# Expert logits from the reads, and one GpSimd chain for two normalisations, in a mixture-of-experts block on one core

## What is computed

```python
    def _L0_ffn_ref(x, gate_w, w1, b1, w2, b2):
        logits = jnp.einsum('bsd,ed->bse', x, gate_w)
        probs = jax.nn.softmax(logits, axis=-1)
        topk_probs, topk_idx = jax.lax.top_k(probs, TOP_K)
        ...
        out = jnp.sum(y * topk_probs[..., None], axis=-2)
        return out
    x = L0_attn_out
    x = x + _L0_attn_ref(_layernorm(x, axis=-1), L0_attn_W_write, L0_attn_W_read, L0_attn_decay, L0_attn_log_alpha)
    x = x + _L0_ffn_ref(_layernorm(x, axis=-1), L0_ffn_gate_w, L0_ffn_w1, L0_ffn_b1, L0_ffn_w2, L0_ffn_b2)
```

## Time and profile before

| | us |
|---|---|
| median of 3 runs | 563.22 (561.47 to 564.38) |
| profiled execution | 562.67 |
| its span in the trace | 560.9 |
| TensorE busy | 530.1 (95%) |
| VectorE busy | 448.4 (80%) |
| ScalarE busy | 338.3 (60%) |
| GpSimd busy | 246.9 (44%) |

### The profile page before, as it was taken

The page is one execution under the profiler, slowest core; times in us unless marked ns, Lnnn a source line. Parts: engine busy times, 40 slices in busy tenths (PEclk is TensorE's granted clock), DMA queues, the critical chain, the costliest instruction groups (busy, mean ns, idle before and its releaser), DMA issues.

```text
span 560.9 us, 17645 instructions
## 1 busy us (share of the span) xinstructions
PE 530.1 (95%) x5234; PEld 415.3 (74%) x5234; DVE 448.4 (80%) x1375; ACT 338.3 (60%) x856; POOL 246.9 (44%) x291
## 2 busy tenths in 40 slices
PE   7799899999999999999999999999999999999991
PEld 7677778778786777777777777777777777777770
DVE  4889999999987689868768787688777777778861
ACT  6899989898745876445545554455544544545540
POOL 5625778888746084523223233223322333322433
PEclk9999999999998999999999999999999999999997
DMA  5576867777345396433263364343344454344323
GB/s 161 201 229 225 258 185 234 210 222 231 126 105 129 87 216 101 71 60 62 51 103 56 53 105 77 63 68 61 61 63 79 78 78 75 68 64 67 63 37 36
DMA packets 85096, 63.33 MB, mean 113 GB/s; under 512 B 54224, under 2 KB 77392, under 8 KB 85008
## 3 DMA queue, kind: packets, MB, share of 16 engines
q1 hardware_dynamic: 71328, 43.94, 32.3%
q0 software_dynamic: 13392, 18.27, 17.3%
q10 hardware_dynamic: 288, 0.00, 0.0%
HBM read 37.56 MB, written 24.62 MB: 111 GB/s over the span
## 4 chain that ended last, share of the span: by engine, by line
PE 77%; DVE 10%; issue 4%; DMA 3%; ACT 2%; POOL 1%; SPq 1%; POOLq 0%; DVEq 0%; ACTq 0%
PE psum L1697 32%; PE psum L1712 21%; PE psum L1714 10%; PE psum L1509 3%; DVE weights L874 2%; PE psum L1592 2%; PE psum L1573 2%; PE psum L1599 2%; PE psum L1520 2%; DVE arena L1052 1%; PE psum L1559 1%; DMA arena<-sent_rows 1%; PE psum L1612 1%; PE psum L1496 1%; DVE arena L1063 1%
## 5 line engine op out<-in xcount | busy, mean ns | idle before, releaser
L1697 PE MATMUL psum<-arena,weights 128*128 128x256 f16 (+1 forms) x2208 | 279.7, 249 | 1.1 <-DVE arena L1316 1.0
L1697 PEld LDWEIGHTS psum<-arena,weights 128*128 x2208 | 187.4, 98 | 79.3 <-issue 4.1
L589 POOL DMA_INDIRECT out<-arena,tile_in x71 | 115.0, 1619 | 233.4 <-DVE arena L1343 126.9
L1712 PE MATMUL psum<-weights,arena 128*128 x556 | 211.7, 381 | 0.0
L826 ACT ACTIVATE arena<-psum,b_cur 128x256 f32<-128x256 f32 (+1 forms) x368 | 131.4, 423 | 129.9 <-PE psum L1697 115.6
L1714 PE MATMUL psum<-weights,arena 128*128 x556 | 152.0, 273 | 0.0
L1327 DVE TENSOR_TENSOR arena<-arena 128x512 f16<-128x512 f32 x142 | 98.5, 694 | 10.8 <-ACT arena L843 6.3
L559 POOL DMA_INDIRECT sent_rows<-arena,tiny x64 | 65.4, 1022 | 35.5 <-issue 17.8
L1323 DVE CAST arena<-arena 128x512 f16<-128x512 f32 x126 | 53.5, 424 | 8.8 <-ACT arena L826 8.5
L1712 PEld LDWEIGHTS psum<-weights,arena 128*128 128x128 f16 x556 | 54.4, 98 | 5.0
L1714 PEld LDWEIGHTS psum<-weights,arena 128*128 128x128 f16 x556 | 54.5, 98 | 4.6
(11 more groups left out here) (199 smaller groups left out, 642.9 us busy)
## 6 DMA issues: line engine op xcount, KB each, us to landing
weights<-in_experts SPq DMA_DIRECT2D x32, 512.0 KB, 4.8
arena<-sent_rows SPq DMA_DIRECT2D x100, 64.0 KB
arena<-in_b SPq DMA_DIRECT2D x46, 128.0 KB, 3.2
arena<-in_x SPq DMA_DIRECT2D x16, 256.0 KB, 3.4
out<-arena SPq DMA_DIRECT2D x16, 256.0 KB, 4.1
arena<-sent_rows SPq DMA_DIRECT2D x84, 32.0 KB
sent_rows<-pad SPq DMA_DIRECT2D x7, 265.0 KB, 4.6
tile_in<-sent_rows SPq DMA_DIRECT2D x71, 4.5 KB, 2.6
```

What stands on the lines that cost most here:

```text
L589: pool.indirect_dma_start(out=out, out_offset=bass.IndirectOffsetOnAxis(ap=at_u, axis=0), in_=yout[:, u % 4], in_offset=None, compute_op=A ...
L1697: last = pe.matmul(ps_h[:, f % 2, mm * n:(mm + 1) * n], w1_of(e_of[i], k, lo, per * (f - GROUP[i]) + mm), turned[:, i % 2, part, k, 0:n], ...
L1712: pe.matmul(to, h_hi[:, z % 4, at], w2_of(e_of[t], m), start=(m == 0), stop=(m == MF - 1), skip_group_check=True)
```

## The change

The logits no longer come from the second normalised rows. Since a row's mean and factor are the same for all its channels, they are a per-row factor times x1 times the gate with each expert's mean over the channels taken off (the centred gate). x1 times that gate splits in two: the reads times (W_read.T times the gate), which becomes eight more columns of `project`; and x + xn, which is a per-row factor (`sides`) times xn, so xn in f16 halves times the gate in f16 halves (`gate_x`), scaled by ScalarE (`scale_gate`). VectorE adds the two. The second factor goes into the exponential as its scale. So logits, choice and scatter come one step earlier (`LAG = 4`), and `turn_normed`, `score_experts` and `normed_transposed` are gone. At the start four small steps prepare the gate: `mean_gate`, `centre_gate`, `gate_in_halves`, `gate_through_reads`, `read_gate`, and one more load of 256 KB, W_read by rows.

GpSimd's two chains become one, of four columns instead of two, which waits for the first moments of chunk n and for the second of chunk n-3. Two small instructions (`roots`, `sides`) follow it.

The diff, cut to what the prediction speaks of:

```diff
-LAG = 5
+LAG = 4
...
+            sp.dma_start(gateT[:], gate_w).then_inc(gate_in, 16)
             sp.dma_start(third_x, both(x_rows, 2)).then_inc(third_in, 16)
             sp.dma_start(ww_words, w_write.rearrange("p k d -> p (k d)")).then_inc(proj_in, 16)
-            sp.dma_start(wrT[:], w_read).then_inc(read_in, 16)
-            sp.dma_start(gateT[:], gate_w).then_inc(gate_in, 16)
-            sp.dma_start(b1T[:], b1).then_inc(gate_in, 16)
+            sp.dma_start(wr_rows, w_read_rows).then_inc(rows_in, 16)
+            sp.dma_start(wrT[:, :, 0:D], w_read).then_inc(read_in, 16)
+            sp.dma_start(b1T[:], b1).then_inc(b1_in, 16)
...
-                        pool.tensor_scalar(ve, moments[:, :, 1], EPS, None, ALU.add)
-                        pool.tensor_scalar(shift, moments[:, :, 0], -1.0, None, ALU.mult).then_inc(S[mid], 1)
-                        reached(pool, mid, m)
-                        pool.tensor_tensor(rs, ve, minus_half[:].to_broadcast([P, B]), ALU.pow).then_inc(S[end], 1)
-                        reached(pool, end, m)
-                        pool.tensor_tensor(shift, shift, rs, ALU.mult).then_inc(S[last], 1)
-                if active(n, 5):
-                    m = n - 5
+                if active(n, 0) or active(n, 3):
+                    both_kinds = slice(0 if active(n, 0) else B, 2 * B if active(n, 3) else B)
+                    count = both_kinds.stop - both_kinds.start
+                    if active(n, 0):
+
+                        reached(pool, "moments1_done", n)
+                        reached(pool, "res_done", n - 2)
+                    if active(n, 3):
+
+                        reached(pool, "moments2_done", n - 3)
+                        reached(pool, "xm_done", n - 5)
+                        reached(pool, "exp_done", n - 5)
+                    got, ve = moments_all[:, both_kinds], variances[:, both_kinds]
+                    rs, shift = factors[par][:, both_kinds], shifts[par][:, both_kinds]
+                    pool.tensor_scalar(ve, got[:, :, 1], EPS, None, ALU.add)
+                    pool.tensor_scalar(shift, got[:, :, 0], -1.0, None, ALU.mult).then_inc(S["taken"], 1)
+                    reached(pool, "taken", n)
+                    pool.tensor_tensor(rs, ve, minus_half[:].to_broadcast([P, count]),
+                                       ALU.pow).then_inc(S["factors_done"], 1)
+                    reached(pool, "factors_done", n)
+                    pool.tensor_tensor(shift, shift, rs, ALU.mult).then_inc(S["shifts_done"], 1)
+                if active(n, 0):
+                    reached(pool, "gate_x_done", n - 4)
+                    pool.tensor_tensor(roots[:], variances[:, 0:B], rs1[par], ALU.mult).then_inc(S["root_done"], 1)
+                    reached(pool, "root_done", n)
+                    pool.tensor_scalar(sides[:, n % 4], roots[:], 1.0 / WSCALE, 1.0 / WSCALE, ALU.mult,
+                                       ALU.add).then_inc(S["side_done"], 1)
+                if active(n, 4):
+                    m = n - 4
...
+            def scale_gate(m):
+
+                reached(a, "gate_x_ps", m)
+                reached(a, "state_done", min(m, NCH - 2))
+                reached(a, "side_done", m)
+                reached(a, "logit_done", m - 1)
+                for b in range(B):
+                    last = a.activation(gate_x_part[:, b], ps_gate_x[:, b], ACT.Copy, scale=sides[:, m % 4, b:b + 1])
+                last.then_inc(S["gate_x_done"], 1)
 
...
-                a.activation(shifted, shifted, ACT.Exp).then_inc(S["exp_done"], 1)
+                reached(a, "factors_done", m + 3)
+                for b in range(B):
+                    last = a.activation(shifted[:, b], shifted[:, b], ACT.Exp, scale=rs2_of(m)[:, b:b + 1])
+                last.then_inc(S["exp_done"], 1)
...
-                if active(n, 5):
-                    exponential(n - 5)
+                if active(n, 3):
+                    scale_gate(n - 3)
+                if active(n, 4):
+                    exponential(n - 4)
...
             def logits(m):
 
-                reached(v, "logit_ps", m)
+                reached(v, "proj_ps", m)
+                reached(v, "gate_x_done", m)
                 reached(v, "top_at_done", m - 1)
-                v.tensor_copy(logit, ps_logit).then_inc(S["logit_done"], 1)
+                v.tensor_tensor(logit, ps_gate_read, gate_x_part[:], ALU.add).then_inc(S["logit_done"], 1)
...
                 if active(n, 3):
                     residual(n - 3)
+                    logits(n - 3)
+                if active(n, 3):
+                    residual_stats(n - 3)
+                    residual_moments(n - 3)
                 for j in splits(n)[0:1]:
                     split_low(j)
-                if active(n, 3):
-                    residual_stats(n - 3)
-                if active(n, 5):
-                    weigh_gates(n - 5)
-                if active(n, 3):
-                    residual_moments(n - 3)
+                if active(n, 4):
+                    weigh_gates(n - 4)
                 if active(n, 2):
                     weigh_scores(n - 2)
-                if active(n, 5):
-                    place(n - 5)
                 if active(n, 4):
-                    logits(n - 4)
+                    place(n - 4)
...
+            def centre_gate():
+
+                v.wait_ge(gate_mean_ps, 1)
+                v.tensor_tensor(gateT[:], gateT[:], ps_gate_mean.unsqueeze(1).to_broadcast([P, KD, E]),
+                                ALU.add).then_inc(gate_centred, 1)
+
+            def gate_in_halves():
+
+                v.wait_ge(gate_centred, 1)
+                v.tensor_scalar(gate16[:, 0], gateT[:], WSCALE, None, ALU.mult).then_inc(gate_halves, 1)
+                v.wait_ge(gate_halves, 1)
+                v.scalar_tensor_tensor(out=gate16[:, 1], in0=gateT[:], scalar=WSCALE, in1=gate16[:, 0], op0=ALU.mult,
+                                       op1=ALU.subtract).then_inc(gate_halves, 1)
+
+            def read_gate():
+
+                v.wait_ge(wr_gate_ps, 1)
+                v.tensor_copy(wrT[:, :, D:D + E], ps_wr_gate).then_inc(wr_gate_done, 1)
...
+            def mean_gate():
+
+                pe.wait_ge(gate_in, 16)
+                pe.wait_ge(mean_set, 1)
+                for k in range(KD):
+                    last = pe.matmul(ps_gate_mean, minus_mean, gateT[:, k], start=(k == 0), stop=(k == KD - 1))
+                last.then_inc(gate_mean_ps, 1)
...
+            def gate_through_reads():
+
+                pe.wait_ge(gate_centred, 1)
+                pe.wait_ge(rows_in, 16)
+                for k in range(KD):
+                    for j in range(KD):
+                        last = pe.matmul(ps_wr_gate[:, k], wr_rows[:, j, k * P:(k + 1) * P], gateT[:, j],
+                                         start=(j == 0), stop=(j == KD - 1))
+                last.then_inc(wr_gate_ps, 1)
+
+            def gate_x(m):
+
+                s = m % 2
+                reached(pe, "gate_x_done", m - 1)
+                reached(pe, "state_done", m - 1)
+                reached(pe, "xlo_done", m)
+                if m == 0:
+                    pe.wait_ge(gate_halves, 2)
+                for b in range(B):
+                    for at, (k, x, w) in enumerate(three):
+                        last = pe.matmul(ps_gate_x[:, b], xnT[:, x, s, b, k, 0:P], gate16[:, w, k],
+                                         start=(at == 0), stop=(at == len(three) - 1))
+                last.then_inc(S["gate_x_ps"], 1)
...
+                reached(pe, "logit_done", m - 1)
...
+                        last = pe.matmul(ps_both[:, b], readsT[:, s, b, k, 0:P], wrT[:, k], start=(k == 0),
                                          stop=(k == KD - 1))
                 last.then_inc(S["proj_ps"], 1)
...
+            mean_gate()
             weigh(0)
             values(0)
             reads(0)
             states(0)
+            gate_through_reads()
             full_steps(step, 3)
-            turn_normed(NCH - 3)
+            gate_x(NCH - 2)
             values(NCH - 1)
             weigh(NCH - 1)
             project(NCH - 2)
-            score_experts(NCH - 3)
+            gate_x(NCH - 1)
             reads(NCH - 1)
-            rank(NCH - 4)
+            rank(NCH - 3)
...
             project(NCH - 1)
-            turn_normed(NCH - 2)
             pair(2, None)
-            rank(NCH - 3)
-            score_experts(NCH - 2)
+            rank(NCH - 2)
             pair(3, 0)
-            rank(NCH - 2)
+            rank(NCH - 1)
             pair(4, 1)
-            turn_normed(NCH - 1)
             pair(5, 2)
-            score_experts(NCH - 1)
             pair(6, 3)
-            rank(NCH - 1)
```

188 lines of the change are left out of this document (89 added, 99 removed).

## The result

| | kernel before | changed kernel |
|---|---|---|
| median of four runs | 562.35 us | 576.05 us |
| range of the runs | 559.97 to 564.38 | 571.25 to 577.94 |
| profiled execution, its span | 562.67, 560.9 | 575.97, 573.9 |
| mean granted clock of the profiled execution | 0.990 | 0.967 |

The ratio is 1.0233, 95% interval 1.0191 to 1.0275: slower by 2.3%. The forecast was 564.9 with a range of 559.5 to 569.5, so the result lies outside, within 1 us of a rival that had been given 5%. That its number comes so close is luck, as the account behind the experiments shows: only about half of what was missed is that rival's.

The account below looks back on a forecast made before the run. A loop through four engines was taken to bound stage one's two-piece steps, VectorE its three-piece steps, TensorE stage two. Terms +1.8 +0.5 +0.3 +1.05 -1.85 -0.1 gave +1.7, 564.9 us with the median's 0.55; range 559.5 to 569.5.

Parts of the forecast that it names:

- the clock falls in stage one: Rival: TensorE idle about 1.9 us ahead of reads halves its clock, +1 to +2 in 12 steps, 577 or more; chance 0.05.
- the three-piece steps: Stage-one chunks with three weight pieces, set by VectorE's work: stats and moments wait, 0.17 a step, +0.5 for three.
- the two-piece pitch: Time between residual starts in stage-one steps with two weight pieces: 9.9 us instead of 9.73, +1.05 over seven.
- the handover: From stage one into stage two, TensorE-bound but for a 1.20 us wait: less logit and transpose work, sum -1.85.
- start: Kernel's beginning: transposes behind new gate matmuls +1.2, GpSimd instructions +0.2, first step's logits and chain +0.4; sum +1.8.
- the signs named: Expected in the profile: pitches near 9.9 and 10.6, GpSimd's first instruction over 1 us, TensorE idle 1.5 to 2 us.
- w: Extra cost of GpSimd's power at four columns over two, in its joint chain; taken as 0.35 us.
- R: Start of VectorE's `residual` in a two-piece step; the first low-half split was to end 3.05 us after it.
- r: Start of ScalarE's `reads_high` in a two-piece step; `residual` was to start 2.92 us after it.
- Double power: Rival: GpSimd's four-column power costs twice the two-column 0.71, pitch 10.25, total 568; chance 0.20.
- TensorE's relief: Rival: with less TensorE work, VectorE's bare 9.29 us sets two-piece steps, total 559.5; chance 0.17.
- No dip: Rival: the half-clock stretch at 177 us stays away because rank waits elsewhere, -1.7, total 563.2; chance 0.08.

Follow-up runs that it names:

- two of its gate's matmuls: Changed kernel with ten of `gate_x`'s twelve matmuls left out; ratio 1.0288 to the kernel before.
- the logits moved: Changed kernel with VectorE's logits behind the residual's moments instead of ahead of its statistics; ratio 1.0167 to the kernel before.
- the gaps filled: Changed kernel plus small bf16 matmuls on ones, ten ahead of states and fourteen ahead of reads each full step; ratio 1.0376 to the kernel before.
- the low half moved: Changed kernel with VectorE's first `split_low` behind the placement; ratio to the kernel before 1.0138 (all steps), 1.0175 (two-piece steps only).
- both moves: Changed kernel with logits behind the residual's moments and, in two-piece steps, first `split_low` behind the placement; ratios 1.0059 and 1.0122 to the kernel before.
- the states held: Changed kernel with logits and first low half moved, TensorE's states also waiting until VectorE has weighed the scores; ratio 1.0166 to the kernel before.
- the low half moved and the fill: Changed kernel with the first `split_low` behind the placement in all steps, plus added matmuls ahead of states and reads; ratio 1.0341 to the kernel before.
- the old work put back: Changed kernel plus, each step, four f32 transposes behind project and four 8-column f32 matmuls between states and reads, without waits; ratio 1.0531 to the kernel before.
- the relieved one: Kernel before with half of the normalised rows' transposes and gate matmuls, and the copy between them, left out; ratio 0.9956 to the kernel before.

## Why the prediction was wrong, step by step

**Two steps failed, with about half of the miss each.** The first is the dismissal of "the clock falls in stage one", which I put at 577 or more with a chance of 0.05. I set against it a granted clock of 1.00 in a stretch in which TensorE was busy 45.4 of 51.4 us. That was a mean: before, TensorE's idle time lay in pieces of at most 0.7 us in the two-piece steps, and in that stretch, ahead of the states in its first two steps, in one of 1.29 and one of 0.73, with at most 0.4 elsewhere. The longest, in the kernel before:

```profile
27.28 0.69 PE L1612 MATMUL psum<-arena 128*64 128x64 f32 x16 [1.29 <-ACT arena L693]
```

In the changed kernel's undisturbed two-piece step it lies in two of 0.86 and 1.20 us, 0.69 apart. Among two-piece steps, half-clock stretches were recorded in all profiles but one of the kernels that keep both gaps (the changed kernel, two of its gate's matmuls, the joint chain undone, the logits moved). There were none with the gaps filled, with the low half moved, with both moves, and with the states held as well. But on chips with late results they also came without the two gaps: with the low half moved and the fill, with the old work put back, with twelve matmuls added to the kernel before, and once each in that kernel itself and in the relieved one. That the two gaps bring the clock down is therefore the reading that fits best and not shown; which of TensorE's waits counts stays open. The price was right in kind: at half clock a step took 11.4 to 12.4 us instead of 10.19.

The second is the sum itself, without any fall. The five disturbed pitches of the profiled execution are 11.45, 11.51, 11.35, 12.44 and 11.63; undisturbed, the same pitches are 10.53 and 10.95 (fastest profile), 10.67 (low half moved alone, which leaves the three-piece steps as they are) and twice 10.19. So the falls cost some 5.9 us, and some 7.1 of the 13.0 are there without them; the fastest profile gives 7.3 in the same way (8.6 less 1.3 for its pitches of 11.36 and 11.32). The forecast was +1.7. By this estimate the time without falls would have been about 570.3, still outside the range. The terms that were too small by these 5.4 us are the three-piece steps, the second above all (2.1), the two-piece pitch (2.6) and the handover (0.7), all told below.

**Where the 13 us of the profiled pair went.** The fastest profile (span 569.5, the changed kernel's last run) has no fall in its two-piece steps and serves as the undisturbed one for them.

| step of the sum | forecast | profiled execution | fastest profile |
|---|---|---|---|
| start | +1.8 | +1.80 | +1.43 |
| the next five pitches, the second step's first | +0.5 | +4.75 | +3.66 |
| seven pitches after them | +1.2 | +7.51 | +3.80 |
| last three pitches and all behind | -1.8 | -1.06 | -0.29 |

*Start*: right, and for the reason given, that the transposes wait for `gate_through_reads`: they began at 22.89, ScalarE took them up at 23.55. *`gate_x`* itself was mis-sized: twelve matmuls take 0.46 us, their starts 27 ns apart, not 0.7. The Trainium skill (TensorE: Matmul & The Clock Gate, Wait — 56ns, not 53.3ns?) states that starts never come closer than about 25 ns; the trace agrees, and an estimate by it would have been 0.3 to 0.5.

*The second step* wasn't in the sum. It has three pieces but had taken only 9.26; now 10.53 in the fastest profile, +1.3. ScalarE's `chunk_normalise` (L744) waits there for the joint chain, which waits for the residual's moments, and starts 5.6 us after the residual (31.13 against 25.52); before, its chain needed no residual and it started after 4.0 (28.05 against 24.09). It is the same dependence that I had priced only for two-piece steps.

*Three-piece steps*: 0.17 each forecast; 0.1 and 0.5 in the undisturbed ones of the fastest profile, 0.9 in two with half-clock stretches, which undisturbed take 10.67, 0.25 more than before.

*Two-piece steps*: most of the signs named came, GpSimd's first instruction with 0.97 beside the split, ScalarE's wait of 1.21 for the chain, TensorE idle ahead of the reads. But that idle time was 1.20 us there and 0.86 ahead of the states, where I had 1.5 to 2 in a row; I had not asked what the states wait for. w was 1.04 - 0.72 = 0.32, forecast 0.35. The pitch was 10.19 and not 9.9 by two small terms: `split_low` was left at R + 3.30, not R + 3.05, since stats and moments ended 0.2 later; and R came at r + 3.08, not r + 2.92, since VectorE's queries, and no longer the projection, were last. 0.3 in seven pitches is 2.1 us of error, inside the range by itself.

*Handover and stage two*: I let the wait before the late rank pass as "only lengthens it". It grew from 1.20 to 2.78 us: TensorE's work ahead of it had gone, and VectorE has L1357 (0.68) ahead of the last residual. The dip came again. Of 1.8 us of gain 0.3 to 1.1 came.

**The rivals.** Double power is excluded by 1.04 (twice 0.71 is 1.42). TensorE's relief did not count, for the reason named: the split begins ahead of the chain. No dip: it came. The chances for faster, same and slower don't follow from the list of cases: two thirds of the forecast's 0.50 and the 0.08 make 0.41 for "same", not 0.53, and 0.42 for "slower", not 0.30.

**What stays open** is the second loss, on three of six chips: results 1.7 us late at full recorded clock. It isn't the joint chain (undone, it was still there), and filled gaps with a recorded clock of 1.00 don't keep it away. Both the order of VectorE's work and the amount of TensorE's bear on it: with the low half moved, or both moves, there were no late results; with the low half moved and 24 matmuls a step added, on the same chip, they were back; ten small matmuls fewer took 1.7 to 0.4, twelve more brought them into three steps of the kernel before, and the old work put back left them. That late results follow how much TensorE does at a stretch is a rival to the order of VectorE's work which no run here decides. Why TensorE is late wasn't found. The Trainium skill (TensorE: Matmul & The Clock Gate, Seeing it yourself) warns that recorded clock events on trn2 have been unreliable; a fall that isn't recorded would fit part of it, but in the filled kernel ScalarE took up the transposes 0.55 us behind the carry's late start, about their modelled distance from `gate_x` at full clock (0.49), so a half clock doesn't explain it all.

## What to carry to other kernels

Work taken off an engine that isn't the bound becomes standing still: look how the remainder falls into pieces, and not at its mean, before calling the clock safe, even if the pattern that counts isn't known. When two chains are joined, price the dependence in every step that had the other chain early, the odd ones too. And keep a VectorE instruction with two SBUF operands away from the moment at which a GpSimd chain starts: here that one place, with the logits', was worth 7 us on one chip and 21 on another in the changed kernel, and nothing in the kernel before.
